# State-space layer and feed-forward block on one core: a slot table of its own for finishing the last chunk but one

## The reference

```python
h = layernorm(x) * (1 + ca) + sa
x = x + ga * selective_ssm(h)          # state h = dA * h + dBx over the 2048 tokens, 16 states
h = layernorm(x) * (1 + cb) + sb
x = x + gb * ffn(h)                    # down(silu(gate(h)) * up(h)), 704 inner columns
```

## Time and profile before

| | us |
|---|---|
| three runs | 359.11, 363.63, 355.99 |
| median | 359.11 |
| profiled execution, its time | 360.38 |
| its span | 358.5 |
| TensorE matmul busy in the span | 265.7 (74%) |
| VectorE | 264.5 (74%) |
| ScalarE | 176.5 (49%) |
| GpSimd | 247.8 (69%) |
| mean granted TensorE clock | 0.819 |

### The profile page before, as it was taken

The page is one execution under the profiler, slowest core; times in us unless marked ns, Lnnn a source line. Parts: engine busy times, 40 slices in busy tenths (PEclk is TensorE's granted clock), DMA queues, the critical chain, the costliest instruction groups (busy, mean ns, idle before and its releaser), DMA issues.

```text
span 358.5 us, 3819 instructions
## 1 busy us (share of the span) xinstructions
PE 265.7 (74%) x1234; PEld 196.9 (55%) x1234; DVE 264.5 (74%) x361; ACT 176.5 (49%) x260; POOL 247.8 (69%) x142
## 2 busy tenths in 40 slices
PE   7940748985446987866999887378986946597996
PEld 7710644954235555644767565357764734465774
DVE  3326599899977899979994999599979958402321
ACT  2352623965453775785355658732454880021410
POOL 2019699999999999999876998995889930010000
PEclk9895586786656798965899989659998995868999
DMA  7529973835535463482328633523574000000001
GB/s 279 166 50 251 240 134 60 119 87 119 121 67 114 66 119 88 94 137 50 103 55 124 105 106 90 119 76 102 99 149 77 1 0 0 2 0 29 30 2 62
DMA packets 33174, 33.10 MB, mean 92 GB/s; under 512 B 14912, under 2 KB 20224, under 8 KB 33152
## 3 DMA queue, kind: packets, MB, share of 16 engines
q1 hardware_dynamic: 32736, 32.01, 41.1%
q10 hardware_dynamic: 416, 0.81, 0.6%
HBM read 30.40 MB, written 2.36 MB: 91 GB/s over the span
## 4 chain that ended last, share of the span: by engine, by line
PE 31%; DVE 30%; POOL 17%; issue 10%; ACT 9%; DMA 2%; DVEq 0%; SPq 0%; POOLq 0%; ACTq 0%
DVE state L865 15%; POOL drv L555 10%; PE side L1128 8%; DVE drv L846 6%; PE sums L1173 5%; POOL drv L568 4%; PE decay L1112 3%; PE side L1096 3%; PE side L1053 3%; ACT gates L711 2%; PE side L1129 2%; ACT decay L723 2%; DMA dtproj_sb<-in_dtprojT 2%; DVE gates L829 2%; PE side L1038 1%
## 5 line engine op out<-in xcount | busy, mean ns | idle before, releaser
L555 POOL TENSOR_TENSOR drv<-u,brow 128x1024 f32<-128x1024 f32 x64 | 153.2, 2411 | 3.2 <-DMA brow<-bc_dram 3.0
L723 ACT ACTIVATE decay<-delta,A 128x512 f32<-128x512 f32 x128 | 87.8, 689 | 101.8 <-DVE state L865 99.3
L865 DVE TENSOR_TENSOR_SCAN state<-decay,last,drv 128x512 f32<-128x512 f32 x96 | 120.1, 1272 | 12.3 <-ACT decay L723 12.2
L1173 PE MATMUL sums<-ident,drv 128*128 128x128 f32 x512 | 79.1, 314 | 0.7 <-POOL drv L568 0.7
L1173 PEld LDWEIGHTS sums<-ident,drv 128*128 128x128 f32 x512 | 69.8, 163 | 12.2 <-issue 8.1
L568 POOL TENSOR_TENSOR drv<-state,crow 128x1024 f32<-128x1024 f32 x28 | 66.1, 2361 | 11.1 <-DVE state L865 11.1
L1147 PE MATMUL rows_ps<-c_parts,sel 64*128 64x512 f32 x36 | 21.1, 587 | 62.0 <-DVE drv L846 57.7
L846 DVE TENSOR_TENSOR drv<-state,rows_ps 128x512 f32<-128x512 f32 x72 | 47.7, 664 | 2.2 <-PE rows_ps L1147 2.1
L1147 PEld LDWEIGHTS rows_ps<-c_parts,sel 64*128 64x128 f32 x36 | 7.7, 214 | 73.7 <-DVE drv L846 62.8
L865 DVE TENSOR_TENSOR_SCAN state<-decay,drv 128x512 f32<-128x512 f32 x32 | 37.9, 1210 | 6.4 <-POOL drv L555 3.4
L1096 PE MATMUL side<-h_hi,ffn_hi 128*128 128x512 f32 x76 | 32.1, 510 | 13.9 <-DVE gates L818 9.9
(11 more groups left out here) (134 smaller groups left out, 306.5 us busy)
## 6 DMA issues: line engine op xcount, KB each, us to landing
brow<-bc_dram SPq DMA_DIRECT2D x32, 512.0 KB, 5.4
crow<-bc_dram SPq DMA_DIRECT2D x12, 512.0 KB, 6.5
resid<-in_x SPq DMA_DIRECT2D x4, 512.0 KB, 6.9
out<-resid SPq DMA_DIRECT2D x8, 256.0 KB, 2.2
crow<-bc_dram SPq DMA_DIRECT2D x4, 256.0 KB, 3.4
gates<-in_wmod ACTq DMA_DIRECT2D x1, 768.0 KB, 5.9
gates<-in_wmod SPq DMA_DIRECT2D x1, 768.0 KB, 7.3
last<-state SPq DMA_DIRECT2D x48, 1.0 KB, 1.9
```

The costliest lines, as they stand in the source:

```text
L555: nc.gpsimd.tensor_tensor(drv[j % RING_DRV][:, :, 0:S], u[:, c % 2, :, 0:S], b.unsqueeze(1).to_broadcast([P, HALVES, S]), ALU.mult).then_i ...
L723: nc.scalar.activation(decay[i % RING_DECAY][:, 0:S], delta[:, c % 2, h, 0:S], ACT.Exp, scale=A[:, h * N + n:h * N + n + 1]).then_inc(deca ...
L865: nc.vector.tensor_tensor_scan(state[j % RING_STATE][:, h, 0:S], decay[i % RING_DECAY][:, 0:S], drv[j % RING_DRV][:, h, 0:S], before, ALU. ...
L1173: ins = nc.tensor.matmul(sums[:, b * D + h * P:b * D + (h + 1) * P], of[:, h, b * P:(b + 1) * P], ident[:, :], is_transpose=True, start=Fa ...
```

## The change

The K tasks of chunk 2 get a table of their own, `CLOSING`, and banks of their own, `PLACE_CLOSING`. The tasks from `st0` to `mixed` come 0.5 to 3 slots earlier, the ups 1 to 2, `silu` 1.5; the `hdn` lie in slots 13 to 15.5 (before: 14.5 to 17.5); the four downs stand together at slot 17, behind the sums of slot 16 (before: two at 18, two at 20), in two banks (1 and 2); `out0` and `out1` at 18. For chunk 3 `h2T` uses banks 0 and 1 in place of 0 and 2. ScalarE loads the silu table at the beginning of step 4, ahead of `xn0` of chunk 3; before, the load stood ahead of that chunk's first gate.

```diff
+CLOSING = {
+    "vector": [
...
+        (13, "K hdn5"), (13.5, "K hdn0"), (14, "K hdn1"), (15, "K hdn2"), (15, "K hdn3"), (15.5, "K hdn4"),
...
+    "gpsimd": [
+        (3, "K rstd"),
...
+    "tensor": [
...
+        (17, "K down0"), (17, "K down1"), (17, "K down2"), (17, "K down3"),
...
+PLACE_CLOSING = {
+    "K h2T": (0, 1), "K gate0": 2, "K gate1": 0, "K gate2": 1, "K gate3": 2, "K gate4": 0, "K mixed": 1,
+    "K up0": 2, "K up1": 0, "K up2": 1, "K up3": 2, "K up4": 0, "K down": (1, 2),
+}
 PLACE_FINAL = {
-    "K h2T": (0, 2), "K gate0": 3, "K up0": 4, "K mixed": 5, "K gate1": 0, "K up1": 2,
+    "K h2T": (0, 1), "K gate0": 3, "K up0": 4, "K mixed": 5, "K gate1": 0, "K up1": 2,
...
+def finish(chunk):
+
+    return FINAL if chunk == NCH - 1 else CLOSING if chunk == NCH - 2 else PLAN
+
+
 def side_tasks(engine, step, slot):
 
-    for plan in (PLAN, FIRST, FINAL):
+    for plan in (PLAN, FIRST, CLOSING, FINAL):
...
-                            kind == "K" and (chunk == NCH - 1) != (plan is FINAL):
+                            kind == "K" and plan is not finish(chunk):
                         continue
...
-                place = PLACE_FINAL if kind == "K" and c == NCH - 1 else PLACE_FIRST if key in PLACE_FIRST and c == 0 \
+                place = PLACE_FINAL if kind == "K" and c == NCH - 1 else \
+                    PLACE_CLOSING if kind == "K" and c == NCH - 2 else PLACE_FIRST if key in PLACE_FIRST and c == 0 \
                     else PLACE
...
             for step in steps:
                 if step == 0:
                     act.wait_ge(A_ready, 1 + HALVES)
+                if step == NCH:
+                    nc.scalar.preload_act_table_set("silu_and_others")
                 for n in range(N):
```

More of the change, by code:

```diff
@@ L102 @@
 }
+CLOSING = {
+    "vector": [
+        (1.5, "K x2"), (1.5, "K st0"), (2, "K st1"), (2, "K agg"), (6.5, "K lo0"), (7, "K lo1"),
+        (13, "K hdn5"), (13.5, "K hdn0"), (14, "K hdn1"), (15, "K hdn2"), (15, "K hdn3"), (15.5, "K hdn4"),
+        (18, "K out0"), (18, "K out1"),
+    ],
+    "gpsimd": [
+        (3, "K rstd"),
+    ],
+    "scalar": [
+        (4.5, "K xn0"), (5, "K xn1"), (6, "K hi0"), (6.5, "K hi1"), (8.5, "K gate0"), (8.5, "K gate1"), (9.5, "K gate2"),
+        (10.5, "K gate3"), (10.5, "K gate4"), (11.5, "K mixed"), (12, "K silu"),
+    ],
+    "tensor": [
[3 rows of a table added]
+    ],
+    "sync": [
+        (18, "K out0"), (19, "K out1"),
+    ],
+}
 FINAL = {
```

## The result

| | before | changed kernel |
|---|---|---|
| median of 4 runs, us | 359.47 | 349.78 |
| lowest to highest | 355.99 to 363.63 | 347.19 to 350.55 |
| profiled execution, its time | 360.38 | 350.55 |
| its span | 358.5 | 348.7 |
| mean granted TensorE clock | 0.819 | 0.853 |

The ratio of the times is 0.974, 95% interval 0.970 to 0.979: faster. The forecast was 349.0 (345.0 to 355.5). The ratio is taken from the undisturbed executions alone and the medians from all, so the two need not divide exactly. VectorE, ScalarE and GpSimd are busy as long as before (263.1, 176.0 and 247.8 us against 264.5, 176.5 and 247.8). TensorE executes as many matmuls (1234) and is busy 258.2 us instead of 265.7, at a higher mean clock. So it is when the engines work that has changed.

The account below looks back on a forecast made before the run. The bound was taken as the chain of waits through TensorE to chunk 3's first product (333.5 to 321.2): 12.3 - 0.85 - 0.85 - 0.5 = 10.1 us off 360.38 gives 350.3, on the median 349.0, range 345.0 to 355.5.

Parts of the forecast that it names:

- Part 1: VectorE's last product of chunk 3: three more hdn ahead (+1.95), a row wait hidden (-0.22), silu stall again 3.8; ends 304.96.
- Part 2: GpSimd with rstd moved ahead of a drive: the lag is taken up by the idle 1.52; 0, at most 0.5.
- Part 3: Last sums of chunk 3 on TensorE, without up3 and up4 between them: end at 307.0 against 309.23, -2.2.
- Part 4: Four downs of chunk 2 start at 307.0 instead of 313.65, take 12.1, end at 319.1, and hide xn.
- Part 5: From transposes' start to second h_hi's end 2.02; chunk 3's first product at 321.2 instead of 333.5, gain 12.3.
- Part 6: Removing ScalarE's 1.28 us silu table load ahead of chunk 3's first gate, hidden by TensorE's work: worth 0.
- Part 7: Deductions: 0.85 for low clock behind the transposes, 0.85 for cold last sums or first downs, 0.5 for ScalarE's gates.
- The 0.85 for a low clock behind the transposes: TensorE's wait of some 1.2 us between transposes and first product: bounds 0 and 1.7, half taken.
- One sign of being wrong: The prediction is wrong if VectorE waits for decays or rows between 270 and 287.
- the low clock at the end of the scan: Rival: TensorE's last sums or first downs run throttled, 2.7 instead of 0.85; 352.2, on the median 350.9; chance 0.25.
- That ScalarE waits for the gates: Rival in the scanning step: TensorE's gate products late at half clock, 4.5 instead of 0.5; median 353.9; chance 0.20.
- That TensorE bounds the whole step: Rival: clock low all through the scanning step, 16.9 lost against 12.3 gained; 365.0, on the median 363.7; chance 0.05.

Follow-up runs that it names:

- e0_after: The changed kernel run once more without an edit: 349.60 us, ratio 0.970 to the kernel before.
- e1: The changed kernel without the silu table preload, the load again ahead of chunk 3's first gate: 348.55 us, ratio 0.966 to the kernel before.
- e2: The kernel before with the silu table preload alone added: 359.83 us, ratio 1.002 to the kernel before.
- e6: The changed kernel with 40 matmuls of zeros added, 32 beside the silu and 8 behind up4: 349.48 us, ratio 0.969 to the kernel before.
- e8: The kernel before with four downs together, two banks, out0 and out1 ahead of h_lo; ups and hdn unmoved, no preload: 358.47 us, ratio 0.999.
- e9: The changed kernel with the sums of rows 12 and 13 ahead of the last spread row: 348.69 us, ratio 0.968 to the kernel before.
- e7: The changed kernel with 40 added matmuls of zeros, and its fourth down and out1 moved behind transposes and h_lo: 349.75 us, ratio 0.970.
- e4: The changed kernel with downs in two pairs, second behind the transposes, one bank for both, out0 behind h_lo: 353.26 us, ratio 0.979.
- e3: The changed kernel with downs in two pairs, second behind the transposes, each in its own bank, out0 ahead of h_lo: 349.57 us, ratio 0.965.
- e10: The changed kernel with sums of rows 12 and 13 ahead of the last spread row and the fourth down behind the transposes: 345.91 us, ratio 0.959.

## Why the prediction was right

The step named as deciding, that the downs waited for the late `hdn` and their bank, and that chunk 3's first product would follow some 12 us earlier, held. With the changed kernel at the full clock that gain was worked out as 12.3; e0_after against before shows 87.10 - 74.64 = 12.46. In the first profile it was 10.86. Less 0.7, because its anchor came later, and less 0.3 for what lies behind the first product, this is 360.38 - 350.55 = 9.8 (forecast 10.1); on the medians it was 9.7. Six more executions of the changed kernel (e0_after) gave a ratio of 0.970 and 11.5 on the medians, so the forecast gain lies between the two measurements of it.

- **Part 1, last product:** forecast +1.73, measured 58.66 - 56.82 = +1.84; silu stall 3.72 (3.8). (The "346 rows" of VectorE are not right: the page counts 361 instructions for either kernel. Nothing rests on it.)
- **Part 2, GpSimd:** 0, and 0. It waited 1.25 longer for the aggregate, and the lag ended where the prediction put it.
- **Part 3, last sums:** forecast -2.2; e0_after 60.94 - 62.85 = -1.9. In the first profile it was only -0.3, because the sums ran at the low clock: 5.23 - 3.71 = 1.5.
- **Part 4, downs:** 309.48 to 321.38 is 11.9 (12.1); `xn` stayed hidden.
- **Part 5:** 323.37 - 321.30 = 2.07 (2.02).
- **Part 6:** 0, shown by e1 in the trace (74.63 and 74.64) and by e2 from the other side.
- **Part 7, the deductions:** together 2.2, measured 12.46 - 10.86 = 1.6 in the first profile, yet made up otherwise. The 0.85 for a low clock behind the transposes was mis-sized: with 0.98 of wait (changed kernel, e0, e1, e6, e8, e9) the products behind it ran at full speed, so 0 was right. The Trainium skill has it so ("TensorE: Matmul & The Clock Gate", section "HAM oscillation — how this bites in real kernels"), since by it only long waits throttle the engine. The low clock behind 1.73 us (changed kernel), 2.39 (e7) and 2.44 (before, e4) goes against the same rule, and there the measurement decides. The 0.85 for cold sums was 1.5 in two profiles of the new table (the first and e7) and nothing in six (e0, e1, e3 to e6). The 0.5 for ScalarE was 0 in the first profile and 0.9 in three runs.

Where the reasoning was thin: I read the 4.11 of the earlier trace rows as what a wait of 2.4 us costs. It cost that in before and in e4, and nothing in e2. So a part of the 12.3, up to 2.4 (87.10 against 84.73), may be a property of the one execution that I started from. Such an error and deductions that were too large have opposite signs, so that the sum came within 0.4 of the medians is in part luck.

One sign of being wrong that the prediction named did appear by its letter: VectorE waits for a decay between 270 and 287, from 285.87 on. It is the silu stall of part 1, moved forward with `silu`, and not a new wait; up to 285.87 VectorE was busy throughout (the window's 16.90 us less the stall's 1.33 are the 15.57 in its row).

Of the rivals, the low clock at the end of the scan is what the first profile shows, at 1.5 instead of 2.7; the wait ahead of the sums was enough for it. That ScalarE waits for the gates occurs at 0.9 instead of 4.5, with a clock that was low for some 6 us only (0.83, 0.50, 0.53 in e3). That TensorE bounds the whole step was not seen.

Open stays in which executions the clock falls behind the wait ahead of the last sums. It fell after 1.73 (first profile) and 2.39 (e7), and not after 2.08 to 2.37 in the six others.

## What to carry to other kernels

Where a new stage starts behind an old one's leftovers, look first at what makes the leftovers late: here the early ups and `hdn` gave 8.6 us, a bank of its own with an early `out0` removed a wait of 2.4, and the grouping of the downs gave 0.25. Fill a wait of TensorE with work that is due anyway (the sums of rows 12 and 13, 1.2 us) and leave just enough behind the transposes to cover the way back over ScalarE (one down, 1.25 us). These two gains are read from the traces; in the times only both together (e10) stand out. One profile isn't enough to price a clock: compare two executions of the same kernel from a common anchor before blaming an edit.

## What the runs showed of the hardware that was not expected

The same wait of 2.44 us was followed by ten downs in 4.11 (before), 4.63 (e4) and 2.43 (e2), and before and e2 have the same work ahead of it. Ahead of the last sums the clock fell behind the wait in two profiles of eight. Behind 0.98 us it never fell (six profiles); behind 4.43 us the ten downs were slow in all three (4.61, 3.88, 3.88 in before, e2 and e8). 64 and 16 matmuls of filler ahead of a wait of 2.39 did not keep the clock up behind it (0.55). A low clock in the middle of the scanning step moved its end by 0.9 us where it lay on the first gates (0.83, 0.50, 0.53 per 3 us in e3), and by nothing where it was a little later and shorter (0.72, 0.71 in e0).
